# Toeplitz rows of four blocks staged over all partitions in a state-space and recurrence kernel

## The reference

```
conv = conv_b + sum(x_pad[:, k:k + L, :] * cond[k] for k in range(128))     # causal, 128 taps per feature
B_t, C_t = softplus((conv @ Wp + bp)[..., :N]), tanh((conv @ Wp + bp)[..., N:])
u = x @ Ws + bs
state = decay * state + dt * B_t * u_t ;  y_t = C_t * state                 # over 128 steps
x = x + y @ Wo + bo
h = tanh(h @ Wh + x_t @ Wx + b)                                             # 128 steps, h starts as cond
x = x + hs
```

## Time and profile before

| | |
|---|---|
| median of 3 runs | 1177.9 us (1176.81 to 1179.24) |
| the profiled execution | 1177.63 us, of which the span is 1175.8 us |
| PE busy | 1157.7 us, 98% of the span |
| PEld, DVE, ACT, POOL busy | 82%, 59%, 48%, 30% |
| DMA moved | 130.12 MB, 34.7% of the 16 DMA engines' span |
| DMA share in the first 8 of 40 slices of 29.4 us | 9, 8, 8, 8, 7, 7, 7, 7 tenths, then 1 to 2 |

### The profile page before, as it was taken

One profiled execution on the slowest core, in us unless ns is written; L12 is line 12 of the kernel. 1 busy time (PEld: TensorE's weight loads), 2 busy tenths in 40 slices (PEclk: granted clock), 3 DMA queues, 4 the chain that ended last, 5 costly groups with the idle time before them and its releaser, 6 DMA issues.

```text
span 1175.8 us, 16134 instructions
## 1 busy us (share of the span) xinstructions
PE 1157.7 (98%) x5984; PEld 969.3 (82%) x5984; DVE 697.0 (59%) x1110; ACT 569.6 (48%) x836; POOL 350.8 (30%) x200
## 2 busy tenths in 40 slices
PE   7899999999999999999999999999999999999997
PEld 7899999975788888888888888888888888888886
DVE  6566767667555555565565665555556556555553
ACT  3555665575354454535454545445354445454431
POOL 4300005022133333333333333333333333333330
PEclk9999999999999999999999999999999999999999
DMA  9888777712022232222222222222222222222202
GB/s 298 251 285 288 253 256 246 249 37 81 1 72 72 74 99 87 89 80 71 71 71 71 71 71 71 71 71 90 91 86 90 71 71 71 71 71 72 72 36 72
DMA packets 73746, 130.12 MB, mean 111 GB/s; under 512 B 3888, under 2 KB 32048, under 8 KB 73712
## 3 DMA queue, kind: packets, MB, share of 16 engines
q1 hardware_dynamic: 73712, 129.65, 34.7%
HBM read 96.08 MB, written 33.55 MB: 110 GB/s over the span
## 4 chain that ended last, share of the span: by engine, by line
PE 96%; DVE 2%; DMA 1%; POOL 0%; issue 0%; ACT 0%; POOLq 0%; SPq 0%; DVEq 0%
PE bank L836 10%; PE bank L844 10%; PE bank L845 10%; PE bank L830 10%; PE bank L848 10%; PE bank L829 10%; PE bank L755 10%; PE bank L770 5%; PE bank L884 5%; PE bank L805 3%; PE bank L811 3%; PE bank L819 2%; PE bank L820 2%; PE bank L784 2%; PE bank L786 2%; PE bank L783 2%
## 5 line engine op out<-in xcount | busy, mean ns | idle before, releaser
L399 POOL TENSOR_TENSOR x_lo<-x_f,x_hi 128x512 fp32r<-128x512 f32 x128 | 161.7, 1293 | 588.0 <-ACT x_hi L490 588.0
L517 ACT ACTIVATE h_f<-z_f 128x512 f32<-128x512 f32 x128 | 80.9, 632 | 296.5 <-DVE z_f L702 296.5
L844 PE MATMUL bank<-wh_hi,hT_hi 128*128 128x512 f32 x512 | 200.6, 392 | 0.0
L845 PE MATMUL bank<-wh_lo,hT_hi 128*128 128x512 f32 x512 | 200.0, 391 | 0.0
L830 PE MATMUL bank<-wx_lo,x_hi 128*128 128x512 f32 x512 | 199.7, 390 | 0.0
L829 PE MATMUL bank<-wx_hi,x_hi 128*128 128x512 f32 x512 | 199.6, 390 | 0.0
L711 DVE TENSOR_TENSOR hT_lo<-bank,hT_hi 128x512 fp32r<-128x512 f32 x128 | 88.5, 692 | 186.8 <-ACT hT_hi L521 186.8
L702 DVE TENSOR_TENSOR z_f<-bank,b_rows 128x512 f32<-128x512 f32 x128 | 88.5, 692 | 131.9 <-PE bank L848 128.6
L393 POOL TENSOR_TENSOR x_lo<-x_f,x_hi 128x2048 fp32r<-128x2048 f32 x32 | 147.7, 4615 | 1.4 <-PE bank L755 1.3
L755 PE MATMUL bank<-ring 128*128 128x128 f32 x1024 | 137.6, 280 | 8.1 <-DMA ring<-x_rev 7.3
L836 PE MATMUL bank<-wx_hi,x_lo 128*128 128x512 f32 x512 | 144.7, 404 | 0.3 <-POOL x_lo L399 0.3
(11 more groups left out here) (83 smaller groups left out, 1637.6 us busy)
## 6 DMA issues: line engine op xcount, KB each, us to landing
ring<-x_rev SPq DMA_DIRECT2D x64, 512.0 KB, 5.2
x_f<-x_dtb SPq DMA_DIRECT2D x32, 1024.0 KB, 8.2
out<-x_f SPq DMA_DIRECT2D x31, 1024.0 KB, 5.5
ring<-hankel SPq DMA_DIRECT2D x44, 512.0 KB, 4.1
ring<-hankel SPq DMA_DIRECT2D x20, 128.0 KB, 4.6
wx_f<-Wx SPq DMA_DIRECT2D x1, 1024.0 KB, 8.2
wh_f<-Wh SPq DMA_DIRECT2D x1, 1024.0 KB, 8.0
out<-x_f SPq DMA_DIRECT2D x4, 256.0 KB, 2.2
```

The source lines that it names most:

```text
L399: nc.gpsimd.tensor_tensor(x1_lo[:, c], x1_f[par][:, c], f(x1_hi[:, c]), ALU.subtract)\
L517: nc.scalar.activation(h_f[:], z_f[:], ACT.Tanh).then_inc(h_ready, 1)
L844: nc.tensor.matmul(z, hT_hi[:, k], wh_hi[:, k], start=False, stop=False)
L845: nc.tensor.matmul(z, hT_hi[:, k], wh_lo[:, k], start=False, stop=False)
```

## The change

The 32 loaded rows of blocks 0 to 19 no longer go into the ring. They go into a new buffer `t_low`, two rooms of 4 KB per partition, in memory that `wx_f` takes later. One room holds the rows of four blocks: block 4k in partitions 0 to 31, block 4k + 1 in 32 to 63, and so on. All four quarters of a Toeplitz matrix are then copied from the room into the slot: POOL copies quarter 3 (all 128 columns) where it copied quarter 2, DVE quarter 2 (96) where it copied quarter 1, ACT quarters 1 and 0 (64 and 32) where it copied quarter 0.

The first four blocks are loaded one by one as before. The rows of the later ones are loaded ahead: with block n, for n below 16, one DMA brings a quarter of what the blocks 4k to 4k + 3 need, k = n // 4 + 1: the feature pair j = n % 4 of each of the four blocks, 128 KB. A copy of block n from 4 on waits until all four of these DMAs have landed and, new, until block n - 4 is convolved, since it writes into that slot. SP gains a wait: before it loads into a room again (n from 4 on), the copies that read that room must be done on all three engines. The quarters stand in the same order in all blocks and the host reorders nothing.

```diff
+            t_low = sb(early, "t_low", [P, 2, CH * P])
+        def toeplitz_lows(k, j):
+            return bass.AP(hankel.tensor, (4 * k * (CH // 2) + j) * 4 * P + 2 * (P - Q),
+                           [[CH // 2 * 4 * P, 4], [2, Q], [1, 2 * TIME]])
+        def low_room(k):
+            return t_low[:, k % 2].rearrange("p (j k) -> p j k", j=CH // 2)
-        def quarter(n, q):
-            at = 3 - q if n % 2 else q
-            return slice(Q * at, Q * (at + 1))
+        def quarter(q):
+            return slice(Q * q, Q * (q + 1))
         def shift_to(n, q):
-            return t_part(n % RING)[quarter(n, q), :, (3 - q) * Q:P]
+            return t_part(n % RING)[quarter(q), :, (3 - q) * Q:P]
         def shift_from(n, q):
-            return t_part(n % RING)[quarter(n, 3), :, 0:(q + 1) * Q]
+            low = t_low[:, n // 4 % 2].rearrange("p (j l i) -> p j l i", j=CH // 2, i=2)
+            return low[quarter(n % 4), :, 0:(q + 1) * Q]
...
             def load_ring(n, slot):
-                if n < SHIFTED:
-                    sp.dma_start(t_rows[quarter(n, 3)], toeplitz_low(n)).then_inc(t_loaded[slot], DMA)
-                else:
+                if n < 4:
+                    sp.dma_start(low_room(0)[quarter(n)], toeplitz_low(n)).then_inc(first_low[n], DMA)
+                k = n // 4 + 1
+                if k < SHIFTED // 4:
+                    if k > 1:
+                        sp.wait_ge(shifted_pool, 4 * (k - 1))
+                        sp.wait_ge(shifted_dve, 4 * (k - 1))
+                        sp.wait_ge(shifted_act, 4 * (k - 1))
+                    sp.dma_start(low_room(k)[:, n % 4], toeplitz_lows(k, n % 4)).then_inc(lows_loaded[k], DMA)
+                if n >= SHIFTED:
                     sp.dma_start(t_rows, toeplitz(n)).then_inc(t_loaded[slot], DMA)
                 sp.dma_start(x_part(slot), x_rev[:, bass.ds(n * CH, CH), :]).then_inc(x_part_loaded[slot], DMA)
...
# POOL; ACT and DVE alike
-                pool.wait_ge(t_loaded[slot], DMA * (n // RING + 1))
-                nc.gpsimd.tensor_copy(shift_to(n, 2), shift_from(n, 2)).then_inc(shifted_pool, 1)
+                pool.wait_ge(first_low[n] if n < 4 else lows_loaded[n // 4], DMA if n < 4 else 4 * DMA)
+                if n >= RING:
+                    pool.wait_ge(conv_done, CH // PER_BANK * (n - RING + 1))
+                nc.gpsimd.tensor_copy(shift_to(n, 3), shift_from(n, 3)).then_inc(shifted_pool, 1)
...
+                nc.scalar.copy(shift_to(n, 1), shift_from(n, 1))
                 nc.scalar.copy(shift_to(n, 0), shift_from(n, 0)).then_inc(shifted_act, 1)
...
-                nc.vector.tensor_copy(shift_to(n, 1), shift_from(n, 1)).then_inc(shifted_dve, 1)
+                nc.vector.tensor_copy(shift_to(n, 2), shift_from(n, 2)).then_inc(shifted_dve, 1)
```

More of the change, by code:

```diff
@@ L88, in build @@
         hT_hi = sb(ctx, "hT_hi", [P, KC, BATCH], F32R)
+        with ExitStack() as early:
+            t_low = sb(early, "t_low", [P, 2, CH * P])
         with ExitStack() as unsplit:
@@ L181, in build @@
         x_part_loaded = [sem(f"x_part_loaded{i}") for i in range(RING)]
+        lows_loaded = [sem(f"lows_loaded{i}") for i in range(SHIFTED // 4)]
+        first_low = [sem(f"first_low{i}") for i in range(4)]
         t_zeroed = sem("t_zeroed")
@@ L336, in shift @@
             def shift(n):
-                slot = n % RING
                 if n < RING:
@@ L420, in shift @@
             def shift(n):
-                slot = n % RING
                 if n < RING:
                     act.wait_ge(t_zeroed, n + 1)
-                act.wait_ge(t_loaded[slot], DMA * (n // RING + 1))
+                act.wait_ge(first_low[n] if n < 4 else lows_loaded[n // 4], DMA if n < 4 else 4 * DMA)
+                if n >= RING:
+                    act.wait_ge(conv_done, CH // PER_BANK * (n - RING + 1))
+                nc.scalar.copy(shift_to(n, 1), shift_from(n, 1))
                 nc.scalar.copy(shift_to(n, 0), shift_from(n, 0)).then_inc(shifted_act, 1)
@@ L543, in zero @@
             def zero(slot):
-                nc.vector.memset(t_part(slot)[quarter(slot, 0), :, 0:3 * Q], 0.0)
-                nc.vector.memset(t_part(slot)[quarter(slot, 1), :, 0:2 * Q], 0.0)
-                nc.vector.memset(t_part(slot)[quarter(slot, 2), :, 0:Q], 0.0).then_inc(t_zeroed, 1)
+                nc.vector.memset(t_part(slot)[quarter(0), :, 0:3 * Q], 0.0)
+                nc.vector.memset(t_part(slot)[quarter(1), :, 0:2 * Q], 0.0)
+                nc.vector.memset(t_part(slot)[quarter(2), :, 0:Q], 0.0).then_inc(t_zeroed, 1)
             def shift(n):
-                slot = n % RING
                 if n < RING:
                     dve.wait_ge(t_zeroed, n + 1)
-                dve.wait_ge(t_loaded[slot], DMA * (n // RING + 1))
-                nc.vector.tensor_copy(shift_to(n, 1), shift_from(n, 1)).then_inc(shifted_dve, 1)
+                dve.wait_ge(first_low[n] if n < 4 else lows_loaded[n // 4], DMA if n < 4 else 4 * DMA)
+                if n >= RING:
+                    dve.wait_ge(conv_done, CH // PER_BANK * (n - RING + 1))
+                nc.vector.tensor_copy(shift_to(n, 2), shift_from(n, 2)).then_inc(shifted_dve, 1)
             zero(0)
@@ L740, in convolution @@
                     if d % CH == 0:
-                        pe.wait_ge(t_loaded[slot], DMA * (n // RING + 1))
+                        if n >= SHIFTED:
+                            pe.wait_ge(t_loaded[slot], DMA * ((n - SHIFTED) // RING + 1))
                         if n < SHIFTED:
@@ L917, in halves @@
         return np.concatenate([a, a], axis=0)
-    x_rev = x.transpose(1, 2, 0)[::-1].copy()
-    for n in range(1, SHIFTED, 2):
-        block = x_rev[:, n * CH:(n + 1) * CH]
-        block[:] = block.reshape(4, Q, CH, BATCH)[::-1].reshape(P, CH, BATCH)
     arrays = {
-        "x_rev": x_rev,
+        "x_rev": x.transpose(1, 2, 0)[::-1],
         "x_dtb": x.transpose(2, 1, 0),
```

## The result

The changed kernel takes 1192.9 us (median, 1192.27 to 1193.16), the kernel before beside it 1178.6. The ratio is 1.0125, with a 95% interval of 1.011 to 1.014: 14.3 us or 1.2% slower. Forecast were 1190, range 1177 to 1199, and slower at 0.79.

A forecast was written before the change was run, and what follows sets the result against it. Loading was taken to bound the first chunk, PE the rest. Block 15's x landing 13.1 us later, less 1.1 at the chunk's end, gave +12.0: 1189.6 on the profiled 1177.63, forecast as 1190, range 1177 to 1199.

The forecast's parts named there:

- What bounds the chunk: First chunk of features: bound by loading at 309 GB/s, PE bounds what follows, so only there can the change move time.
- The shape of the load: New DMA in the first chunk: 4 outermost in the source confines it to four engines; +12, against +1.2 over sixteen.
- The price of a block: First chunk: load work per block on the four loaded engines, taken as 2.9 us, where all sixteen had 1.76.
- its own count of 3.08: Packet count per block on a loaded engine: 32 small at 0.055 plus 8 large at 0.165 us.
- two bounds: Limits on a block's load time: 2.77 us from the best rate seen, 3.3 us from a pair of such DMAs.
- SP's added wait: Before block 4: SP goes on at 12.8, engines could idle some 0.6 us; counted as covered on four engines.
- The end of the chunk: Before the first transpose: copy-out no longer waits behind a copy of Toeplitz rows; idle about 1.0 for 2.07, gain 1.1 us.
- The dip of the clock: PE's granted 0.68 behind the idle stretch at the chunk's end: may go, but left in; 3.4 us at half level cost 1.7.
- The sum: Loaded engine's work to block 15: its x lands at 52.1 for 39.0, 13.1 later, less 1.1 at the end: +12.0.
- A load spread over all engines: Rival for the first chunk: loads ahead run on all 16 engines, +1.2 us, 1179; chance 0.18.
- The faster one: Rival for the first chunk: spread loads writing all partitions exceed 309 GB/s; 4.6 us less at 340, 1173; chance 0.07.
- PE's clock: Rival: four engines, and idling between blocks halves the clock for half of 12 later blocks; 5.4 us more, 1195; chance 0.13.

## Why the prediction was right, and where it was off

**What bounds the chunk.** Right: loading did, and the time moved in the first chunk alone.

**The shape of the load.** Right, and shown three times over: by 192 missing completion packets, by the share of 0.25 while only the loaded engines had work, and by the two experiments on the outermost count (16 engines 1.0023, 4 engines 1.0125, 2 engines 1.0293). The rule cited from the Trainium skill (DMA: Bandwidth & Descriptors, Why a DMA increments its semaphore by 16 and not by 1) holds here for 4 and for 2 outermost. That it is the lowest-numbered engines no row shows.

**The price of a block.** 2.9 us taken, 2.87 measured. The 55 ns for a packet of 1 KB was too high: with 1.32 us kept for the large packets it is (2.87 - 1.32) / 32 = 48 ns, and 42 with two engines. The two paces alone give (3.98 - 2.87) / 32 = 35 ns for each packet added, so the large packets may well cost more than their 165 ns here; the runs don't separate the two. The forecast took 2.9, below its own count of 3.08, as a value between two bounds, so that it came out so close is in part luck.

**SP's added wait.** This step failed. The text said that it "is covered here, as the loaded engines have work until about 16.5 us"; it had SP go on at 12.8, from when DVE's copy for block 3 started in the kernel before. But that copy's own rows now stood behind three loads on the same four engines and landed near 16, and SP went on at 17.47. A wait was priced with the time of its releaser before the change, though the change itself delays the releaser. That the loaded engines have work for so long was about right: by the forecast's own terms until 0.75 + 1.9 + 1.76 + 1.3 + 4 x 2.9 = 17.3, not 16.5, and by the trace until about 18. With SP back at 12.8 that would have covered the wait; with SP back at 17.47 it didn't. Four rooms took 2.9 us off by the medians and 1.7 on the traces.

**The end of the chunk.** The wait was right: 0.88 left, gain 1.2 for 1.1. The dip of the clock was left in and went: the stretch behind the transposes ran at the granted level 1.00 in place of 0.68. That is a miss in the other direction: from the first transpose to the third (L770 before, L795 after) it is 48.58 - 43.34 = 5.24 us before, 62.64 - 58.85 = 3.79 after, 1.45 less on the profile.

**The sum.** 12.0 forecast, 14.3 measured: 12.0 + 2.9 for SP's wait - 1.45 for the clock is 13.5, with 0.8 left. By the traces it is 12.0 + 1.7 - 1.45 = 12.3, with 1.7 left of the 14.0 us ahead of the recurrences. That rest lies at the start of the chunk. The sum puts the `x` of block 4 at 0.75 + 1.9 + 1.76 + 1.3 + 5 x 2.9 = 20.2, but even with four rooms block 4 starts at 23.08; the pace of 2.83 for 2.9 gives 0.8 of these 2.9 us back. What makes the start longer stays open; it isn't the order in SP's queue, since with `x` first block 4 still starts at 22.36. (The 24 packets that the sum gives `wp_f` are 32 of 768 bytes per engine in the trace, some 0.4 us at most.) So the `x` of block 15, forecast for 52.1, landed at 55.9, and the first transpose, forecast for 55, started at 58.85. The clock's miss had the opposite sign, which made the forecast look better than its parts: that 1190 came so near is in part luck.

**The rivals.** A load spread over all engines could be run as a kernel of its own, though with loads into 32 partitions: 1.0023 with SP's wait, 1.0010 without, against 1.2 us (1.0010) forecast. The faster one, of loads that write all partitions from sixteen engines, was not tested: no kernel here has such loads, and the 299 GB/s with loads of one block say nothing of it. PE's clock did fall once, with block 4 after the 3.71 us of idling (two blocks in 5.47), but not in the regular gaps of 0.3 to 1.4 us; the mean in the chunk is 0.95, not the half of the blocks that this rival took. What the rival describes did come with two outermost, where the gaps were longer and the mean was 0.86 and 0.84.

## What to carry to other kernels

Look at the outermost count of both sides of a DMA before its bytes: the engines that carry it follow from what divides both, and a transfer that looks evenly spread over 128 partitions can sit on four engines and hold up every large transfer queued with it. To check it in a profile, count the completion packets, or find a stretch in which only that transfer is left and read the share. And price an added wait with the time at which its releaser comes after the change, not before it.

## What the runs showed of the hardware

A load engine that runs nearly alone moves some 25 GB/s in packets of 1 and 4 KB (99 GB/s with four, 51 to 53 with two); all sixteen together held 309, 19 each. So four engines are hurt less than a count of packets at the crowded price says.

SP takes longer to issue a load with 4 outermost: 0.55 us for each of those from 17.47 us on in the changed kernel that are not held up, 0.32 for a load of one block with 32 outermost.

Whether the half clock follows an idle stretch isn't given by its length alone: 2.07 us of idling were followed by it in the kernel before, 2.33 us before block 4 with loads of one block too (granted 0.59 from 21.2 to 24.6 us). But 2.16 us at the end of the chunk in the kernel with four outermost and `x` first were not (granted 1.00 from 57.5 to 62.8 us), nor were 1.75 us or 0.88 us at that place in other kernels. What decides between 2.07 and 2.16 stays open.
